# Second expert layer: matmuls with the high part of the hidden units first, those with the low part last

## What is computed

```
logits = x @ router_w + router_b
probs = jax.nn.softmax(logits, axis=-1)
top_v, top_i = jax.lax.top_k(probs, TOP_K)          # TOP_K = 2, 8 experts
gate = jnp.einsum('td,edi->eti', x, gate_w) + gate_b[:, None, :]     # d = 256, i = 512
up = jnp.einsum('td,edi->eti', x, up_w) + up_b[:, None, :]
h = jax.nn.silu(gate) * up
expert_out = jnp.einsum('eti,eid->etd', h, down_w) + down_b[:, None, :]
y = jnp.einsum('te,etd->td', weights, expert_out)
```

## Time and profile before

| | |
|---|---|
| median of three timed runs | 447.67 us (446.89 to 449.02) |
| the profiled execution | 449.13 us |
| its span, first to last instruction | 447.3 us |
| mean granted TensorE clock | 0.842 |
| TensorE busy | 349.4 us (78%) |
| VectorE busy | 343.0 us (77%) |
| GpSimd busy | 246.7 us (55%) |
| ScalarE busy | 208.2 us (47%) |
| second layer L884, 468 matmuls | 58.8 us busy |
| first layer L863, 468 matmuls | 113.7 us busy |

### The profile page before, as it was taken

The page is one execution under the profiler, slowest core; times in us unless marked ns, Lnnn a source line. Parts: engine busy times, 40 slices in busy tenths (PEclk is TensorE's granted clock), DMA queues, the critical chain, the costliest instruction groups (busy, mean ns, idle before and its releaser), DMA issues.

```text
span 447.3 us, 12542 instructions
## 1 busy us (share of the span) xinstructions
PE 349.4 (78%) x4491; PEld 217.5 (49%) x4492; DVE 343.0 (77%) x693; ACT 208.2 (47%) x343; POOL 246.7 (55%) x267
## 2 busy tenths in 40 slices
PE   0077878767778769679247899999999999999981
PEld 0076634444454445534013466666666666666640
DVE  6988699799999999966794577677677677677660
ACT  1047547847857757633900243443443443443430
POOL 5616357566656757661485165555565565555541
PEclk9997566578758577569767999999999999999995
DMA  8410002323321412603793234334323323324322
GB/s 197 118 45 1 2 1 74 119 97 96 97 94 51 137 51 95 176 17 79 205 305 136 89 48 61 59 47 63 55 47 58 59 47 59 59 47 62 57 23 23
DMA packets 24963, 35.30 MB, mean 79 GB/s; under 512 B 4992, under 2 KB 18304, under 8 KB 24160
## 3 DMA queue, kind: packets, MB, share of 16 engines
q1 hardware_dynamic: 16256, 24.46, 18.1%
q0 software_dynamic: 7488, 10.23, 14.3%
q10 hardware_dynamic: 1184, 0.14, 0.2%
HBM read 25.39 MB, written 9.44 MB: 78 GB/s over the span
## 4 chain that ended last, share of the span: by engine, by line
PE 55%; DVE 20%; issue 10%; ACT 5%; POOL 4%; DMA 2%; DVEq 1%; SPq 0%; POOLq 0%; ACTq 0%
PE bank L863 22%; PE bank L884 13%; PE bank L874 4%; DVE s_exp L1295 2%; PE bank L531 2%; DVE att L1329 2%; PE bank L851 2%; PE bank L759 2%; DVE v_exp L1348 2%; PE bank L646 2%; POOL v_exp L486 2%; DVE maxes L1288 2%; DVE q_exp L1363 2%; DMA token_rows<-z_stack 1%; DVE z_pair L1282 1%
## 5 line engine op out<-in xcount | busy, mean ns | idle before, releaser
L863 PE MATMUL bank<-w_exp,w_stage 128*128 x468 | 113.7, 379 | 1.2 <-DVE w_stage L1541 0.2
L515 POOL DMA_INDIRECT out_dram<-w_stage,gate x39 | 62.1, 1592 | 7.6 <-issue 7.6
L863 PEld LDWEIGHTS bank<-w_exp,w_stage 128*128 128x128 f16 x468 | 45.6, 97 | 41.8 <-issue 4.6
L406 POOL TENSOR_TENSOR w_exp<-w_stage,w_exp 128x1024 f16<-128x1024 f32 (+1 forms) x24 | 51.0, 2129 | 22.1 <-ACT w_exp L1023 22.1
L884 PE MATMUL bank<-w_exp,q_exp 128*128 x468 | 58.8, 276 | 2.1 <-DVE q_exp L1568 2.1
L1551 DVE TENSOR_TENSOR v_exp<-bank,x_rows 128x512 f32<-128x512 f32 x39 | 27.0, 692 | 35.7 <-PE bank L863 35.7
L1128 ACT ACTIVATE w_stage<-w_stage,gate 128x256 f32<-128x256 f32 x39 | 19.8, 508 | 68.8 <-DMA out_dram<-w_stage,gate 35.2
L884 PEld LDWEIGHTS bank<-w_exp,q_exp 128*128 128x128 f16 x468 | 42.3, 98 | 16.9 <-issue 11.6
L505 POOL DMA_INDIRECT w_stage<-token_rows,gate x39 | 39.0, 999 | 17.3 <-PE bank L851 11.8
L514 POOL TENSOR_TENSOR gate<-gate 1x1 f32<-1x1 f32 x39 | 7.1, 183 | 69.3 <-ACT w_stage L1128 68.2
L1120 ACT ACTIVATE q_exp<-bank 128x512 f16<-128x512 f32 x39 | 23.3, 597 | 27.6 <-PE bank L874 27.6
(11 more groups left out here) (248 smaller groups left out, 776.2 us busy)
## 6 DMA issues: line engine op xcount, KB each, us to landing
w_stage<-in_L_ffn_gate_w_dram SPq DMA_DIRECT2D x8, 512.0 KB, 3.4
w_stage<-in_L_ffn_up_w_dram SPq DMA_DIRECT2D x8, 512.0 KB, 3.5
w_stage<-in_L_ffn_down_w_dram SPq DMA_DIRECT2D x8, 512.0 KB, 3.5
x_rows<-in_x_dram SPq DMA_DIRECT2D x8, 256.0 KB, 5.9
out_dram<-x_rows SPq DMA_DIRECT2D x4, 512.0 KB, 5.9
token_rows<-z_stack SPq DMA_DIRECT2D x4, 512.0 KB, 6.0
x_rows<-in_L_ffn_gate_b_dram SPq DMA_DIRECT2D x1, 2048.0 KB, 11.9
z_stack<-in_L_ffn_up_b_dram SPq DMA_DIRECT2D x2, 1024.0 KB, 7.1
```

The costliest lines, as they stand in the source:

```text
L406: pool.tensor_tensor(lo, w_stage[:, k, :], hi, ALU.subtract).then_inc(s["w_lo_done"], 1)
L515: pool.indirect_dma_start(out, bass.IndirectOffsetOnAxis(t_scatter[:, b:b + 1], 0), yw[b % 2], None, compute_op=ALU.add).then_inc(s["y_sca ...
L863: mm = pe.matmul(GU[par][k][:], xs[par][:, c, :], w_exp[:, w * W_EXP + k * W_PIECE + c * FF:][:, bass.ds(e, FF)], start=(n == 0), stop=(n ...
```

## The change

In `down`, the loop over the three products (high with high weights, high with low weights, low with high weights) becomes the outer loop, in the order high, high, low, and the loop over the four pieces the inner one. The function waits for hh_ready where it waited for hl_ready, and for hl_ready only in front of the four matmuls with h_lo. The twelve products are the same; all are summed in the same bank.

```
             def down(b, par, e, first=False):
-                pe.wait_ge(s["hl_ready"], b + 1)
+                pe.wait_ge(s["hh_ready"], b + 1)
                 if not first:
                     pe.wait_ge(s["yadd_ready"], b)
                 n = 0
-                for c in range(4):
-                    for hs, w in ((h_hi, 0), (h_lo, 0), (h_hi, 1)):
+                for hs, w in ((h_hi, 0), (h_hi, 1), (h_lo, 0)):
+                    if hs is h_lo:
+                        pe.wait_ge(s["hl_ready"], b + 1)
+                    for c in range(4):
                         mm = pe.matmul(YB[:, 0:L_COL], hs[par][:, c, :],
                                        w_exp[:, w * W_EXP + 2 * W_PIECE + c * L_COL:][:, bass.ds(e, L_COL)],
                                        start=(n == 0), stop=(n == 11))
```

## The result

The changed kernel takes 443.44 us (median of four runs, 443.33 to 443.84) against 447.51 us for the kernel before on the same chip: a ratio of 0.9906, with a 95% interval of 0.988 to 0.9931. That is 4.1 us faster. The forecast was 9.3 us (438.4), with a range of 436.6 to 441.8. The sign is right, the size is less than half, and the time lies outside the range, close to the 443.6 us that the rival "another pace takes over" was priced at, with a chance of 0.06.

What follows compares the result with a forecast made beforehand. TensorE was taken to bound the expert stage; 5.9 us from the bubble before the second layer, 2.3 from the loop's turns and 1.1 at the end sum to 9.3, giving 438.4 us, range 436.6 to 441.8.

Steps and rivals of the forecast that it cites:

- another pace takes over: Rival: scatter chain's period of 4.65 us lets only 0.08 of each 0.16 us come; 443.6 us, chance 0.06.
- (a): TensorE's bubble before the second layer, 0.16 us in each of 37 blocks, goes: 5.9 us gained.
- (b): Added wait for h_lo before the ninth matmul costs nothing, with 0.83 us of cover.
- (c): Second layer's register instructions on TensorE stay at eight; twelve would need 0.5 us more per block, covered inside the loop.
- (d): At a turn of the loop, TensorE's bubble of 0.29 us goes: 8 turns, 2.3 us gained.
- What is late next: Scatters' period is 4.25 us, below TensorE's new block of 4.57 us, so TensorE stays the bound.
- (e): At the end, the last L514 comes at 437.67 instead of 438.73: 1.06 us gained.
- the low case of the step: In the last block, all twelve matmuls run at the slow clock level; the end gains only 0.4 us.
- The slower rival: Restart behind the added wait isn't hidden, leaving a gap after the eighth matmul: 5.2 us slower, 452.9 us, chance 0.04.
- The turn stays: Rival: a taken loop branch still costs 0.29 us, or twelve register instructions eat the lead; 440.7 us, chance 0.22.
- it doesn't do what it says: Rival: the second layer's bubble comes from register instructions, not h_lo, and stays; about 446 us, chance 0.06.

Runs made afterwards that it cites:

- experiment 3: Kernel before with the new order of the twelve matmuls, but the one wait on hl_ready kept at the top of down: 451.17 us, ratio 1.0079.
- experiment 7: Changed kernel with each gather issued one block sooner, ahead of the scatter it stood behind: 442.99 us, ratio 0.9895.
- experiment 8: Changed kernel with the landing waited for on a second one-word multiplication on GpSimd and gathers one block sooner: 438.96 us, ratio 0.9806.
- experiment 1: Changed kernel with the wait for the previous scatter's landing moved from a sequencer event to a second one-word multiplication on GpSimd: 439.86 us, ratio 0.9821.
- experiment 5: Kernel before with five one-word multiplications instead of one between the wait for the landing and the next scatter's issue: 452.48 us, ratio 1.0095.

## Why the prediction was wrong, point by point

**The bubble before the second layer (a): right.** 0.22 instead of 0.38, in every block without a late gather. **The added wait (b): right**, no gap after the eighth matmul. **Eight register instructions (c): right** in number:

```profile
L886 PEldq FUSED_REGOPS  x8: 46/46/60, 321.7 to 322.6; - x8
```

Their price was looked at too narrowly, though. The step asked whether there would be eight or twelve and not how they fall on the matmuls. Their distance of 0.124 stands in the prediction, and the pitch of 0.110 too; with one for each of the first eight matmuls, the new order costs 0.13 us per block when nothing hides it (experiment 3). Here the lead hid it, as the step said of the twelve, except behind a late gather.

**The turn of the loop (d): right** where the lead is there. It is 1.33 at seven of the eight turns instead of 1.61; at the eighth (345.68), right behind three blocks with late gathers, it is still 1.58. TensorE's own time fell as summed: from the first block's second layer to that of block 36 (the last with transposes of x before it) it was 253.56 to 426.27, 172.7 us; with the gathers out of the way it is 252.63 to 416.87, 164.2 us (experiment 7). That is 8.5 us, where (a) and (d) give 36 x 0.16 + 8 x 0.29 = 8.1 for this stretch.

**The failed step is "What is late next".** It put the period of the scatters at 3.8 + 0.1 + 0.34 = 4.25 us, below TensorE's 4.57. The 0.34 was read from a block in which L514 waited for its data, 323.50 to 323.84. The landing had come 0.49 before L514, at 323.01, so the preparation of the scatter had run beside that wait. The event that waits for it is recorded in the kernel before, from 322 to 324 us, as

```profile
L513 POOLq EVENT_SEMAPHORE  x1: 17/17/17, 323.0 to 323.0; - x1
```

From this landing to this issue it is 323.84 - 323.01 = 0.83: the block that the step read was itself at the minimal distance. The 0.1 and the 0.34 belong to two different situations and can't be added. The right distance is the one from the landing to the next issue, where nothing but the landing is late, and the trace of before has it. GpSimd there, in order of time:

```profile
271.46 1.58 POOL L515 DMA_INDIRECT out_dram<-w_stage,gate  x1 [0.52 <-issue]
...
275.44 0.18 POOL L514 TENSOR_TENSOR gate<-gate 1x1 f32<-1x1 f32 x1 [1.10 <-DMA out_dram<-w_stage,gate]
276.13 1.58 POOL L515 DMA_INDIRECT out_dram<-w_stage,gate  x1 [0.51 <-issue]
```

Here L514 was released by the landing, and from L514 to L515 it is 0.69. Issue to issue is 4.67 us, with nothing in between but the landing: the chain's true period, 0.1 above TensorE's new 4.57 and just below its old 4.73. With that, the cap would have been plain: 38 periods of 4.67 from the first scatter of before (256.67) give a last one at 434.1 instead of 439.07, a gain of 4.9 us and a time of 442.7. The rival had the mechanism and, with a guessed period of 4.65, nearly the time; it got 0.06 because the wrong 4.25 spoke against it. That its 443.6 lies within 0.2 us of the measured time is in part luck. No row gives its 4.65; the prediction's own sum with the slowest landing is 4.45. It set the 4.65 against blocks of 4.73 alone and left out the turns: 38 periods of 4.65 against 38 of 4.80 give 5.7 us, not 3.0. And it added 1.1 at the end, which belongs to the same chain.

**The end (e)** went as described in kind: the last L514 follows the landing, 0.14 behind it. But the 1.06 holds the same mistake, a distance of 0.34 from L514 to the issue, as it was when the data came last; behind a landing it is 0.65 there. From the landing of the last scatter but one to the issue of the last it was 1.36 us before and is 0.79 now, so the end gives 0.6, and that is part of the chain's 4.7, not something beside it. The last second layer takes 1.62 us at a granted clock of 1.00, behind 1.11 us of idle time; before it took 2.43, behind 1.86 us of idle time, with a mean granted clock of 0.59 from 435.0 to 437.5. So the low case of the step, all twelve at the slow level, didn't occur.

**The slower rival** didn't occur: no gap stands at the wait inside the accumulation group. **"The turn stays"** and **"it doesn't do what it says"** are excluded by the rows above. The Trainium skill's figure of about 131 ns per 512-column matmul ("TensorE: Matmul & The Clock Gate", Back-to-back issue gap) is not what any run here shows: six take 1.30 us, 216 ns each, also where nothing holds TensorE back (experiments 7 and 8).

What stays open: what GpSimd's sequencer does in the 0.42 us that the moved wait gives back. Experiments 1 and 5 show that it runs beside work and waits of the engine and isn't started while an event holds the sequencer, not more.

## What to carry to other kernels

When a stall is removed from the bounding engine, the next bound is a loop's period, and each loop through a DMA (issue, landing, next issue) has to be read where that loop itself was the last to arrive; durations from iterations in which something else was later overlap and give a sum that is too small. A wait that a sequencer executes as an event can hold back the preparation of what stands behind it (0.83 against 0.41 us here), so it pays to try the wait that comes last on an engine instruction. An order that asks for one register instruction per short matmul needs a lead of the sequencer, and without the lead it costs more than it seems to move.

## What the runs showed of the hardware that was not expected

- From the landing of one indirect scatter to the issue of the next: 0.83 us with the wait as an event on GpSimd's sequencer, 0.41 us with the wait on a one-word multiplication, 1.06 us with five multiplications (0.77 us together) behind the event.
- TensorE's address instructions come 0.124 us apart, so that eight matmuls of 256 columns with one each run at 0.124 instead of 0.109 us when the sequencer has no lead (experiment 3).
- In blocks of the changed kernel with a late gather (331.30) the second layer took 1.43 instead of 1.31 us as well, with its first matmuls at the same 0.124: the wait had cost TensorE's sequencer its lead.
